# A fused kernel whose step is put in another order: rows turned behind the router on VectorE, the control product in front of the LoRA products on TensorE, output stores moved up on ScalarE, powers rotated by pairs

## The reference, cut to what is computed

```python
# layer 0: convolution with a kernel of 64 complex modes for each head
dtA = A * dt[:, None]
Cs = Cc * (jnp.exp(dtA) - 1.0) / A
K = 2.0 * jnp.einsum('hn,hnl->hl', Cs, jnp.exp(dtA[:, :, None] * arange(L))).real
y = irfft(rfft(u * mask) * rfft(K)) + u * mask * D;   x = x + y * mask
# layer 1: projection, router, LoRA of the two best experts
base = einsum('btd,od->bto', x, W);   logits = einsum('btd,ed->bte', x, Wr) + bias
topw, topi = top_k(logits, 2);        gates = softmax(topw) at topi
x = x + base + 2.0 * einsum('bter,bte,eor->bto', einsum('btd,erd->bter', x, A), gates, B)
```

## Time and profile before

| | |
|---|---|
| median of 3 runs | 644.51 us |
| the profiled execution | 645.27 us |
| its span, first to last instruction | 643.5 us |
| TensorE / VectorE / ScalarE busy | 96% / 81% / 68% |
| granted TensorE clock, mean | 0.991 |
| DMA, mean over the span | 67 GB/s |

### The profile page before, as it was taken

One profiled execution on the slowest core, in us unless ns is written; L12 is line 12 of the kernel. 1 busy time (PEld: TensorE's weight loads), 2 busy tenths in 40 slices (PEclk: granted clock), 3 DMA queues, 4 the chain that ended last, 5 costly groups with the idle time before them and its releaser, 6 DMA issues.

```text
span 643.5 us, 12483 instructions
## 1 busy us (share of the span) xinstructions
PE 619.5 (96%) x3439; PEld 592.7 (92%) x3439; DVE 524.1 (81%) x1560; ACT 437.9 (68%) x949; POOL 34.7 (5%) x61
## 2 busy tenths in 40 slices
PE   4798989999999999999999999999999999999997
PEld 4697989999999999999999999999999999999997
DVE  7887778888888888888888888888888888887741
ACT  5788687686676768667685867668576867764421
POOL 2241000000000000000000000000000000000000
PEclk9798999999999999999999999999999999999999
DMA  6531424443233444433334443232444432331212
GB/s 182 165 106 34 75 42 75 74 73 61 52 53 56 72 73 73 73 56 54 56 54 73 73 73 66 56 58 41 73 73 73 73 58 52 51 59 42 42 33 66
DMA packets 137856, 43.41 MB, mean 67 GB/s; under 512 B 127304, under 2 KB 132208, under 8 KB 137840
## 3 DMA queue, kind: packets, MB, share of 16 engines
q1 hardware_dynamic: 132960, 27.39, 25.6%
q10 hardware_dynamic: 4880, 15.83, 10.0%
HBM read 26.35 MB, written 16.85 MB: 67 GB/s over the span
## 4 chain that ended last, share of the span: by engine, by line
DVE 32%; PE 23%; issue 22%; ACT 16%; SPq 3%; ACTq 2%; DMA 1%; DVEq 1%
DVE state L970 11%; PE pmg L1313 11%; PE pc L1248 8%; ACT swapped L555 7%; DVE xt L1011 5%; ACT state L563 2%; DVE s_lo L999 2%; DVE zo_lo L922 2%; PE pmg L1300 1%; DVE gate L1044 1%; ACTq L606 1%; ACT t_hi L539 1%; ACT zo_hi L546 1%; ACT result L600 1%; DVE angle L787 1%
## 5 line engine op out<-in xcount | busy, mean ns | idle before, releaser
L1313 PE MATMUL pmg<-w_hi,y_hi 128*128 128x384 f32 (+1 forms) x768 | 263.2, 343 | 1.7 <-DVE y_lo L1017 1.7
L1313 PE MATMUL pmg<-w_hi,y_lo 128*128 128x384 f32 (+1 forms) x768 | 259.9, 338 | 0.0
L1313 PE MATMUL pmg<-w_lo,y_hi 128*128 128x384 f32 (+1 forms) x768 | 259.7, 338 | 0.0
L1313 PEld LDWEIGHTS pmg<-w_hi,y_hi 128*128 128x128 f32 x768 | 144.2, 188 | 2.7 <-issue 2.1
L1313 PEld LDWEIGHTS pmg<-w_hi,y_lo 128*128 128x128 f32 x768 | 144.3, 188 | 0.5
L1313 PEld LDWEIGHTS pmg<-w_lo,y_hi 128*128 128x128 f32 x768 | 144.2, 188 | 0.0
L555 ACT ACTIVATE swapped<-state 64x128 f32<-64x128 f32 x192 | 59.3, 309 | 66.3 <-DVE state L970 64.9
L970 DVE SCALAR_TENSOR_TENSOR state<-swapped,scan_tab,state 128x192 f32<-128x192 f32 (+1 forms) x240 | 73.7, 348 | 16.5 <-ACT swapped L555 12.1
L600 ACT ACTIVATE result<-pmg 128x384 f32<-128x384 f32 (+1 forms) x96 | 41.7, 449 | 39.4 <-PE pmg L1300 37.2
L1017 DVE TENSOR_TENSOR y_lo<-xt,y_hi 128x1024 fp32r<-128x1024 f32 x32 | 39.2, 1225 | 20.6 <-ACT y_hi L582 19.2
L970 DVE SCALAR_TENSOR_TENSOR state<-state,scan_tab 128x64 f32<-128x64 f32 x180 | 51.3, 327 | 3.1
(11 more groups left out here) (208 smaller groups left out, 1063.5 us busy)
## 6 DMA issues: line engine op xcount, KB each, us to landing
out<-result ACTq DMA_DIRECT2D x60, 256.0 KB, 4.3
rows<-in_x SPq DMA_DIRECT2D x224, 64.0 KB, 3.6
toe<-kpad SPq DMA_DIRECT2D x30, 128.0 KB, 4.8
rows<-in_x SPq DMA_DIRECT2D x8, 256.0 KB, 3.9
rows<-in_L_cond_W SPq DMA_DIRECT2D x3, 512.0 KB, 6.5
result<-in_L_cond_W SPq DMA_DIRECT2D x3, 512.0 KB, 6.4
w_rows<-in_L_cond_W SPq DMA_DIRECT2D x2, 512.0 KB, 4.8
result<-in_L_cond_A SPq DMA_DIRECT2D x1, 512.0 KB, 5.9
```

The lines of the kernel that those rows point to most:

```text
L1313: ins = nc.tensor.matmul(pm[:, n, 0:o1 - o0], y[s][:, c, :], w[:, c, o0:o1], start=(c == 0 and y is y_hi and w is w_hi), stop=(c == CH - 1 ...
```

## The change: what it does

Nothing is computed in another way, and every product, split and scan stands in both kernels; the order on three engines is different, and some waits go with it.

- VectorE: `turn_rows` for pair i+2 stood at the end of the step before, and now stands right behind `route`, in front of `s_lo` and `u_lo`. The kernel column (`kernel_column`) and the split of `t` take the places of the two `hold` copies in `route`. `split_gated` stands in the place of the `hold` in `merge`, behind the wait for `conv_done`. `rotate_powers` (four heads, odd step) becomes `rotate_pair`, two heads in each step. The first pair of the scan's operations stands in front of the split of `y`, and the first of them waits for the even chunks alone (`evens_ready`), not for the swapped ones too.
- TensorE: `control` stands in front of `add_loras`.
- ScalarE: `split_states` is now at the start of the step that needs it. `ratios`, `evacuate` j = 2 and `store` stand together, in front of `turns_of` / `swap_powers`, `turn_powers` (odd step) and `split_turned`. The table load for the exponential is moved from the even step's scan to the odd step, in front of `ratios`. `copy_states` stands in front of `split_y` and of the two evacuations, and takes the swapped halves from SBUF.
- GpSimd: one more small copy for each pass (`stage_second`).

```diff
@@ -438,13 +442,19 @@
                 vec.tensor_copy(scan_tab[:, :, :], tab[:, A_RE:AA_IM + 1, bass.ds(g * DUO, DUO)]
                                 ).then_inc(scan_staged, 1)
+            def stage_second(g):
+                vec.tensor_copy(second_tab[:, :], tab[:, CC_IM, bass.ds(g * DUO + 2, 2)]).then_inc(second_staged, 1)
+
             pool.wait_ge(scan, SCAN * 2)
             stage_scan(1)
+            stage_second(2)
             with pool.Fori(1, LOOPS) as b:
-                pool.wait_ge(z2_ready, b + 2)
+                pool.wait_ge(z2_turned, 2 * b - 1)
                 stage_gen(b + 2)
                 pool.wait_ge(scan, SCAN * (2 * b + 2))
                 stage_scan(b + 1)
+                pool.wait_ge(z2_turned, 2 * b)
+                stage_second(b + 2)
             pool.wait_ge(scan, SCAN * (2 * LOOPS + 2))
             stage_scan(LOOPS + 1)
...
@@ -560,8 +570,9 @@
                 act.wait_ge(v_full, i + 1)
                 if not first:
                     act.wait_ge(slo_ready, i)
-                nc.scalar.activation(state[:, :, EVENS, :], v_psum[:, :, EVENS, :], ACT.Copy)
-                swap_state(i, slice(0, CARRIED - 1, 2), v_psum).then_inc(v_copied, 1)
+                nc.scalar.activation(state[:, :, EVENS, :], v_psum[:, :, EVENS, :], ACT.Copy).then_inc(evens_ready, 1)
+                act.wait_ge(evens_ready, i + 1)
+                swap_state(i, slice(0, CARRIED - 1, 2), state).then_inc(v_copied, 1)
             def swap_odd(b, m, n):
...
@@ -705,40 +716,41 @@
             nc.scalar.activation(warm[:, :], phase[:, 0:1], ACT.Exp)
             for n in range(3):
                 swap_odd(0, 3, n)
-            split_states(0, 3)
             def step(b, m, rows_left=True, kernels=True):
                 split_toe(b, m + 1)
+                split_states(b, m + 1)
                 if rows_left:
                     split_ctr(b, m + 2)
                     split_obs(b, m + 2)
+                if kernels and m == 1:
+
+                    nc.scalar.activation(warm[:, :], phase[:, 0:1], ACT.Exp)
+                ratios(b, m)
                 evacuate(b, m - 1, 2)
-                if rows_left:
-                    split_turned(b, m + 2)
-                ratios(b, m)
+                store(b, m - 1)
                 if kernels and m == 0:
                     act.wait_ge(gen_staged, b)
                     turns_of(None, True)
                 if kernels and m == 1:
                     swap_powers(b + 2)
-                store(b, m - 1)
+                    turn_powers(b + 2, True)
+                if rows_left:
+                    split_turned(b, m + 2)
                 split_gated(b, m)
                 if kernels and m == 0:
                     magnitudes(None, True)
                     waves(b + 2)
-                if kernels and m == 1:
-                    turn_powers(b + 2, True)
+                if rows_left:
+                    copy_states(b, m + 2)
+                split_y(b, m + 1)
+                if rows_left:
+                    swap_odd(b, m + 2, 0)
                 for j in range(2):
                     evacuate(b, m, j)
-                split_y(b, m + 1)
                 if rows_left:
-                    copy_states(b, m + 2)
-                    if kernels and m == 0:
-
-                        nc.scalar.activation(warm[:, :], phase[:, 0:1], ACT.Exp)
-                    for n in range(3):
-                        swap_odd(b, m + 2, n)
-                    split_states(b, m + 2)
+                    swap_odd(b, m + 2, 1)
+                    swap_odd(b, m + 2, 2)
             with act.Fori(1, LOOPS) as b:
                 for m in range(2):
...
@@ -932,6 +944,22 @@
                 vec.tensor_tensor(c_lo[:, :, :], ct_psum, c_hi[:, :, :].bitcast(F32), ALU.subtract
                                   ).then_inc(clo_ready, 1)
+            def low_ct(b, m):
+                dve.wait_ge(chi_ready, 2 * b + m + 1)
+                vec.tensor_tensor(c_lo[:, :, :], ct_psum, c_hi[:, :, :].bitcast(F32), ALU.subtract
+                                  ).then_inc(clo_ready, 1)
+
+            def kernel_column(m):
+
+                vec.reduce_sum(k_col[m % 2][:, :], ct_psum[:, :, 0:MODES], axis=mybir.AxisListType.X).then_inc(k_ready, 1)
+
+            def rotate_pair(g, j, scalars):
+                dve.wait_ge(z_swapped, g + 1)
+                for h in (2 * j, 2 * j + 1):
+                    ins = vec.scalar_tensor_tensor(out=Z2[:, h, :], in0=z_swap[:, h, :], scalar=scalars[h - 2 * j],
+                                                   in1=Z2[:, h, :], op0=ALU.mult, op1=ALU.add)
+                ins.then_inc(z2_turned, 1)
+
             def rotate_powers(g, staged):
                 dve.wait_ge(z_swapped, g + 1)
                 for h in range(DUO):
...
@@ -973,9 +1001,10 @@
                             in1=(state if into is None else into)[:, h, chunks, :], op0=ALU.mult, op1=ALU.add)
                     ins.then_inc(scan, 1)
-                dve.wait_ge(v_copied, i + 1)
+                dve.wait_ge(evens_ready, i + 1)
                 add(ODDS, state, slice(0, CARRIED - 1, 2), A_RE, into=v_psum)
                 dve.wait_ge(scan, start + 1)
+                dve.wait_ge(v_copied, i + 1)
                 add(ODDS, swapped, slice(0, CARRIED - 1, 2), A_IM)
                 yield
                 for n in range(2):
...
@@ -1002,11 +1031,11 @@
             def hold():
                 vec.tensor_copy(held[:, :], lang_f[:, :])
-            def merge(b, m):
+            def merge(b, m, behind_conv=hold):
                 i, s = 2 * b + m, m % 2
                 dve.wait_ge(ulo_ready, i + 1)
                 dve.wait_ge(conv_done, i + 1)
-                hold()
+                behind_conv()
                 for h in range(2):
                     ins = vec.copy_predicated(xt[s][:, :, h * SEQS:(h + 1) * SEQS], valid[:, :, :], pc[:, h, :, :])
                 ins.then_inc(merged, 1)
...
@@ -1017,17 +1046,18 @@
                 vec.tensor_tensor(y_lo[s][:, :, :], xt[s][:, :, :], y_hi[s][:, :, :].bitcast(F32), ALU.subtract
                                   ).then_inc(ylo_ready, 1)
-            def route(b, m):
+            def route(b, m, behind_logits=hold, behind_top=hold):
+
                 i = 2 * b + m
                 gate = pm[:, 2, :]
                 base = ROUTER * i
                 dve.wait_ge(gate_done, i + 1)
                 vec.tensor_tensor(logits[:, :], gate[:, L0:L0 + EXPERTS], bias[:, :], ALU.add).then_inc(router, 1)
                 dve.wait_ge(router, base + 1)
-                hold()
+                behind_logits()
                 vec.max(top[:, :], logits[:, :]).then_inc(router, 1)
                 dve.wait_ge(router, base + 2)
-                hold()
+                behind_top()
                 vec.max_index(top_at[:, :], top[:, :], logits[:, :]).then_inc(router, 1)
                 dve.wait_ge(router, base + 3)
                 vec.tensor_copy(top_no[:, :], top_at[:, 0:2]).then_inc(router, 1)
...
@@ -1131,41 +1161,47 @@
             split_gated(0, 1)
             split_rows(0, 3)
             merge(0, 2)
-            rotate_powers(2, False)
+            rotate_pair(2, 0, [gen_scalar(CC_IM, 2, h, False) for h in range(2)])
             scanning = scan_states(0, 3)
             next(scanning)
             split_y(0, 2)
             for _ in scanning:
                 pass
-            turn_rows(0, 4)
             def step(b, m, rows_left=True, kernels=True, ahead=True):
-                split_toe(b, m + 1)
+                toe_split = partial(split_toe, b, m + 1)
                 if rows_left:
-                    split_ctr(b, m + 2)
+                    low_ct(b, m + 2)
                     if m == 1:
                         split_obs(b, m + 2)
                 if kernels and m == 1:
                     powers(b + 2)
-                route(b, m)
+                if rows_left:
+                    route(b, m, partial(kernel_column, m + 2), toe_split)
+                    turn_rows(b, m + 2)
+                else:
+                    route(b, m, behind_top=toe_split)
                 split_states(b, m + 1)
                 if rows_left:
                     split_rows(b, m + 2)
-                split_gated(b, m)
-                if rows_left and m == 0:
-                    split_obs(b, m + 2)
+                    if m == 0:
+                        split_obs(b, m + 2)
                 if kernels and m == 0:
                     angles(b + 2)
-                merge(b, m + 1)
-                if kernels and m == 1:
-                    rotate_powers(b + 2, True)
+                merge(b, m + 1, partial(split_gated, b, m))
+                if ahead and m == 0:
+                    dve.wait_ge(second_staged, b)
+                    rotate_pair(b + 1, 1, [second_tab[:, h:h + 1] for h in range(2)])
+                if ahead and m == 1:
+                    rotate_pair(b + 2, 0, [gen_scalar(CC_IM, None, h, True) for h in range(2)])
+                if rows_left:
```

(20 more changed lines are left out.)

10 lines of the change are left out of this document (8 added, 2 removed).

## The result

| | before | after |
|---|---|---|
| median, same chip | 646.01 us (4 runs, 644.13 to 648.00) | 665.62 us (4 runs, 664.94 to 666.76) |
| span of the profiled execution | 643.5 us | 664.6 us |
| granted TensorE clock, mean | 0.991 | 0.991 |

A forecast was written before the change was run, and what follows sets the result against it. TensorE bounds the kernel, with only 0.56 us of waiting per pass; 643.5 + 15.0 (13 passes at +1.15) - 0.5 = 658.0 span, 659.8 with the 1.8 around it, 659 against the median; range 643 to 665.

The forecast's parts named there:

- the mechanism of the odd step: Odd step: stores delay ScalarE's `z_swap`, Z2 and `u_hi`, so `control` waits for `u_lo`; 1.7 us of waiting, `s_lo` included.
- A: Rival, 0.16 together with D: the stores on ScalarE hold nobody up; pass 37.15 us, time 645.
- B: Rival, 0.09: the old odd-step wait goes and none comes, with earlier logits and cheap stores; pass 36.50, time 637.
- the stores: ScalarE: two store issues hold it for 1.17 us from the evacuation's end to the end of the second issue.
- D: Rival, 0.16 together with A: moving `control` is harmless because the wait for `s_lo` hides it; 644.
- 0.5 us of waiting for `s_lo`: Middle of the odd step's convolution: `s_lo` ends at P+10.5, due at P+10.06; P starts `project` j = 0.
- The even step ... I cost it at nothing.: Even step: `u_lo` ready with 0.3 us to spare, so no cost; if short by 0.3 it adds 4 us.
- ends 1 us before the LoRA matmuls: `gt_lo`, now behind the convolution, ends 1 us before the LoRA matmuls that moved behind `control`, so it has room.
- No wait before, none now: Last steps: no powers there, and no wait before or after the change; no cost.
- the start: Start-up: TensorE's 1.72 us wait for `y_lo` shrinks, 0.4 us gained, plus 0.1 in the first pass.
- rival C: Rival, 0.07: both steps wait, as the even step lacks 0.3 us or stores exceed 1.17 us; 662 to 666.
- the 1.3 us of transposes are gone: VectorE in front of the router: transposes leave, then `c_lo` waits for ScalarE's `s_hi` (0.95) and `c_hi` (0.37).

The follow-up runs named there:

- the fastest kernel: The changed kernel with stores late, transposes back, `gt_lo` early in the even and last step, and `u_hi` right behind the evacuation: 635.86 us, 0.9858 of the kernel before.

## Why the prediction was right or wrong

Forecast 659 us (643 to 665), measured 665.62: slower, as forecast, and by more.

**Right: the mechanism of the odd step.** Forecast and measured, from P: `z_swap` 7.9 and 7.72, Z2 9.2 and 9.01, `u_hi` 10.45 and 10.20, `control` 12.9 and 12.78, the step 19.95 and 19.81. The term on which rivals A and B hung, the stores, was taken at 1.17 and measured 1.35; that it is whole and not half or nothing the hole in both kernels shows. A, B and D fell with it. A's price would not have stood either: a pass of 37.15, where the run with the stores late has 37.74. (D's 644 is 643 by its own terms, 13 x 0.06 and 0.5 off 644.5.)

**Right by two errors that cancel: the length of the odd step.** I said 0.5 us of waiting for `s_lo` and logits at P+5.5; measured were 0.1 and P+5.10, 0.4 early, because the even step ended 0.5 late. From the end of the evacuation to `control` it takes 6.4 and not 6.2, 0.18 of it in the stores. That the sum came out at 19.81 for 19.95 is luck. The run with `gt_lo` early has the even step nearly as forecast, and its odd step takes 20.37: logits P+5.65, `control` at P+13.32 and not 12.9.

**The step that failed: "The even step ... I cost it at nothing."** It takes 18.75, not 18.25, 6.5 us over the 13 passes. The check that I made, of `u_lo` against `control`, nearly held: `u_lo` ended at P+11.14 (forecast 10.95, due at 11.27), and `control` starts at P+11.34. The operand that I did not check there is `gt_lo`. I wrote that it "ends 1 us before the LoRA matmuls", which is so in the odd step, where it stands right behind `u_lo`; in the even one `zo_lo` and two operations on `angle` stand between, 1.6 us, and it ends 0.3 us too late. The same instruction costs the last step 0.76 us (17.55 against 16.79): no `control` stands between convolution and LoRA there to cover it. "No wait before, none now" was said of the last steps without looking at it.

**Also off: the start.** The 0.4 us I counted as gained are not there. TensorE waits for `y_lo` 1.68 us, where it waited 1.72, and gets there at 90.03 where it got there at 89.96:

```profile
90.03 0.44 PE L1351 MATMUL pmg<-w_hi,y_hi 128*128 128x392 f32 x1 [1.68 <-DVE y_lo L1046]
```

**The sum.** From gate transpose to gate transpose, after less before: 13 passes 20.2 us (forecast 15.0), last steps 0.95 (0), start 0 (-0.5): 21.1 us of span against 14.5. Of the missing 6.6 the loop has 5.2: the even step 6.5 more than forecast, the odd step 1.8 less, and the rest mostly in the loop's first pass. This was priced in rival C ("both steps wait", 662 to 666, as "the even step lacks the 0.3 us"), whose size was right and whose named operand was wrong: it was mainly `gt_lo`, with 0.05 for `u_lo`. Against this stands that removing the late `gt_lo` does not help: the pass is then 38.74, with the odd step 0.42 above its forecast and the even one 0.12. So the forecast of 38.2 would have failed without this wait too, and the second term that it had too small is the odd step's path over logits and stores. That the pass hardly changes (38.56 and 38.74) while TensorE's wait moves from one step to the other, and that the odd logits stay within 0.3 us at 23.86 to 24.13 behind the even P in these runs, points to a loop of VectorE and ScalarE that sets the loss; TensorE only waits at different places in it.

**What the prediction did not see at all** is that the transposes had been free. It read "the 1.3 us of transposes are gone" and then, in the same sentence, that `c_lo` must wait for `s_hi` and `c_hi`: 1.3 us. Both numbers stand there, and the conclusion, that the move gains nothing in front of the router and costs its length behind it, was not drawn. It changed no number of the forecast. It is the second half of the cause in the sense of the table above: behind the stores it costs 0.01 us of a pass, and once they are out of the way 0.97.

The clock stayed where it was, as forecast: mean 0.991 in both kernels, and 1.00 from 130 to 600 us in both, with a wait of 1.3 us in each pass after the change.

## What to carry to other kernels

When an instruction is moved out of a chain, ask what its engine would have waited for in its place: where the next one needs another engine's result anyway, the moved work was free there and costs its full length where it goes. Put nothing that only empties a buffer, and DMA issues least of all, in front of an operand that a matmul waits for, and for each matmul that is moved make the table of due times for *all* operands, in each kind of step (odd, even, first, last). Where two chains end at one operand, undo suspects in pairs: alone they looked worth 2 and 11 us, together they were worth 25.

## What the runs showed of the hardware

- Two DMA issues on ScalarE's queue hold the next activation back for 1.35 us from the end of the evacuation ahead: 0.18 to the first issue, 1.13 for both, 0.04 to the activation. So it is at all 24 places between 135 and 600 us, after the change and in the kernel before with the stores early. No row of before showed this. It agrees with the Trainium skill (Perfetto Trace Analysis, Per-engine timelines, HWDGE): the sequencer is free for the next instruction only at the profiled end of such an instruction. The same two issues cost nothing where activations that run long enough stand ahead of them: in the fastest kernel they start at 296.97 and 297.62 while `z_swap` and Z2 run. Behind `u_hi` in the run with the stores late they left 0.34 us idle in the odd step and 0.43 in the even one.
- A DMA issue whose own condition had been met did not pass a waiting `ratio` ahead of it. ScalarE, last step of the kernel before:

```profile
625.89 0.49 ACT L600 ACTIVATE result<-pmg 128x384 f32<-128x384 f32 x1 [3.02 <-PE pmg L1300]
630.63 0.29 ACT L586 ACTIVATE ratio<-top 128x1 f32<-128x1 f32 x1 [4.25 <-DVE top L1028]
630.63 0.47 ACTq L606 DMA_DIRECT2D out<-result  x1
```

  The evacuation that it waits for had ended at 626.38. The run with the stores late shows the same in the even steps: the evacuation ended at P+5.85, `u_hi` waited 1.26 us for its rows until P+8.65, and the first issue behind it started at P+8.87. With the rows there in time (transposes back too) the issues started at P+6.01 and P+6.75, ahead of the `u_hi` (P+7.29) that stands in front of them in the program. The same page of the skill has engine instructions only pushed into a wait queue, by which the issue could have gone at once; in the last step of the kernel before, where the wait stands in the program as an instruction of its own ahead of the activation, the issue started 4.25 us later, together with `ratio`.
- The granted clock of one stretch of the start-up, 50 to 68 us, was 0.91 in the profiled executions of seven kernels here (before and after among them) and 1.00 in five. The first step took 28.8 to 29.5 us in the seven and 27.7 in the five. In the kernel before the clock was at the lower level of 1.2 GHz (granted 0.50) from 56 to 58 us, behind a pause of TensorE at 52 to 53. Whether the edits or chance decide this isn't shown, so a difference of 1 us between two of these kernels is read in the loop and not in the total.
